# Routing tiles of a gated cross-attention and expert block: GpSimd's root, the probability transposes, the list columns and ScalarE's Exp each move within their queues

## What is computed

```python
kv = (ctx @ W_kv.T + b_kv).reshape(B, S, 16, 16, 2)          # k and v, 16 heads of 16
scores = einsum('bshd,bstd->bsht', layernorm(x), k) / 4      # over the heads t of one token
x = x + tanh(g0) * (einsum('bsht,bstd->bshd', softmax(scores), v) @ W_out.T + b_out)
xn = layernorm(x)
probs = softmax(einsum('ntd,ed->nte', xn, gate_w))           # 8 experts
g, m = top_k(probs.transpose(0, 2, 1), 64)                   # each expert takes 64 of 256 tokens
h = gelu(xn[m] @ w1[e]) @ w2[e]
x = x + tanh(g1) * scatter_add(g * h, m)
```

## Time and profile before

| | us |
|---|---|
| median of 3 runs | 764.04 |
| lowest and highest | 762.25, 764.85 |
| profiled execution, its time | 766.51 |
| profiled execution, its span | 764.5 |
| mean granted TensorE clock | 0.912 |

### The profile page before, as it was taken

One profiled execution on the slowest core, in us unless ns is written; L12 is line 12 of the kernel. 1 busy time (PEld: TensorE's weight loads), 2 busy tenths in 40 slices (PEclk: granted clock), 3 DMA queues, 4 the chain that ended last, 5 costly groups with the idle time before them and its releaser, 6 DMA issues.

```text
span 764.5 us, 10848 instructions
## 1 busy us (share of the span) xinstructions
PE 647.5 (85%) x3592; PEld 517.6 (68%) x3592; DVE 630.2 (82%) x894; ACT 388.3 (51%) x882; POOL 579.4 (76%) x497
## 2 busy tenths in 40 slices
PE   5678867453689999984999999859999999999994
PEld 2234433221478888873878888747888889999994
DVE  5899999997999999967999999859999743567672
ACT  5466656432466666733666666535665542323321
POOL 3899989996877999867898889858899833445443
PEclk9877898755699999996999999977999999999998
DMA  6877755230347878764688887536777878899982
GB/s 192 311 237 252 263 203 200 103 132 27 111 152 222 244 231 244 214 182 126 189 243 253 247 232 226 186 89 191 233 225 220 238 227 281 286 306 317 304 252 27
DMA packets 97069, 160.91 MB, mean 210 GB/s; under 512 B 8171, under 2 KB 74486, under 8 KB 97014
## 3 DMA queue, kind: packets, MB, share of 16 engines
q1 hardware_dynamic: 84150, 142.91, 56.1%
q0 software_dynamic: 12288, 16.79, 11.6%
q10 hardware_dynamic: 576, 0.52, 0.2%
HBM read 126.63 MB, written 33.55 MB: 210 GB/s over the span
## 4 chain that ended last, share of the span: by engine, by line
PE 55%; POOL 19%; DVE 8%; DMA 7%; issue 7%; ACT 3%; POOLq 0%; ACTq 0%; DVEq 0%
PE bank L1010 20%; PE bank L991 20%; POOL prod_p L313 9%; DMA out_dram<-ys,ids 7%; POOL tree_a L319 5%; PE bank L918 4%; DVE prod_v L456 3%; PE bank L938 3%; POOL tree_b L319 3%; PE bank L901 2%; PE bank L979 2%; POOL tree_c L319 1%; DVE co L458 1%; PE bank L950 1%; PE bank L927 1%
## 5 line engine op out<-in xcount | busy, mean ns | idle before, releaser
L991 PE MATMUL bank<-xin,w1in 128*128 128x256 f32 x1536 | 210.3, 296 | 5.5 <-DVE xin L592 3.8
L991 PEld LDWEIGHTS bank<-xin,w1in 128*128 128x128 f32 x1536 | 199.5, 202 | 7.2 <-issue 6.8
L1010 PE MATMUL bank<-w2s,hT 128*128 128x256 f32 x768 | 175.4, 382 | 0.0
L379 POOL DMA_INDIRECT out_dram<-ys,ids x64 | 110.0, 1719 | 75.6 <-ACT ys L747 57.9
L1010 PEld LDWEIGHTS bank<-w2s,hT 128*128 128x128 f32 x768 | 142.4, 190 | 17.7
L737 ACT ACTIVATE hT<-bank 128x512 f32<-128x512 f32 x128 | 76.4, 597 | 118.5 <-PE bank L991 118.1
L313 POOL TENSOR_TENSOR prod_p<-kvs,q 128x1024 f32<-128x1024 f32 (+2 forms) x32 | 99.8, 3118 | 13.0 <-ACT q L704 12.9
L458 DVE TENSOR_REDUCE co<-prod_v 128x192 f32<-128x3072 f32 (+1 forms) x32 | 104.6, 3270 | 1.1
L456 DVE TENSOR_TENSOR prod_v<-bank,Ex 128x3072 f32<-128x3072 f32 (+1 forms) x32 | 104.5, 3265 | 0.1
L456 DVE TENSOR_TENSOR prod_v<-bank,q 128x3072 f32<-128x3072 f32 (+2 forms) x32 | 95.5, 2983 | 6.3 <-ACT q L704 6.3
L365 POOL DMA_INDIRECT xg<-xn_scratch,ids x64 | 65.0, 1016 | 46.1 <-DVE ids L582 28.6
(11 more groups left out here) (118 smaller groups left out, 1044.9 us busy)
## 6 DMA issues: line engine op xcount, KB each, us to landing
w1in<-w_parts SPq DMA_DIRECT2D x128, 512.0 KB, 5.4
w2s<-in_L_ffn_w_dram SPq DMA_DIRECT2D x32, 1024.0 KB, 6.2
w_parts<-w1s SPq DMA_DIRECT2D x32, 512.0 KB, 3.4
w1raw<-in_L_ffn_w_dram SPq DMA_DIRECT2D x32, 256.0 KB, 4.3
ct<-in_ctx_dram SPq DMA_DIRECT2D x32, 128.0 KB, 5.3
xt<-in_x_dram SPq DMA_DIRECT2D x32, 128.0 KB, 4.2
out_dram<-x SPq DMA_DIRECT2D x32, 128.0 KB, 4.2
xn_scratch<-xn SPq DMA_DIRECT2D x32, 128.0 KB, 2.7
```

The source lines that it names most:

```text
L379: pool.indirect_dma_start(out=out_rows[:, :], out_offset=bass.IndirectOffsetOnAxis(ap=ids[:, g % 2, p * E + e:p * E + e + 1], axis=0), in_ ...
L991: ins = pe.matmul(HB[k % 2][:, D * f:D * (f + 1)], w1in[:, k, w, c, P * f:P * (f + 1)].bitcast(f32r), xin[:, n % 2, x_, c, :], start=(m == ...
L1010: ins = pe.matmul(dst, hT[:, n % 2, f, cols], w2s[:, n % 2, f, :], start=(f == 0), stop=(f == FC - 1))
```

## The change

Only the order of calls in the routing tiles changes, and one instruction of each choice of tokens goes. GpSimd: rsqrt(s + 1) stands ahead of scores(s). VectorE: residual(s - 1) stands behind Sc, ahead of routes, as in other tiles; the last match_replace of a choice, whose result nobody reads, is left out. ScalarE: take_y stands behind the Exp, and the Exp's table is loaded by a one-column Exp (`exp_warm`) behind make_q. TensorE: prob_transposes stands ahead of hidden(n, 0), and route_columns ahead of outputs(n - 1, 1); in tile 10 prob_transposes stands ahead of co_transposes, and xn_transposes and logits ahead of route_columns. The loops of ScalarE and TensorE are written anew with the routing tiles apart; the order of other tiles is as it was.

```diff
 # GpSimd
             for s in range(NT):
+                if routing(s):
+                    rsqrt(s + 1)
                 scores(s)
-                rsqrt(s + 1)
+                if not routing(s):
+                    rsqrt(s + 1)
 # VectorE
-                if t > 0 and not routing(t):
+                if t > 0:
                     residual(t - 1)
                 if routing(t):
                     routes(t // TG - 1)
...
                 products(hc, Vp, Ev[:, 0:hc, :], co[:, 0:hc * DK], 2 * t + 1, cov_done)
-                if t > 0 and routing(t):
-                    residual(t - 1)
...
-                    dve.max_index(top_i[:, eight], top_p[:, eight], work[:, :])
-                    dve.match_replace(work[:, :], top_p[:, eight], work[:, :], -1.0).then_inc(removed8, 1)
-                    wait_apart(removed8, n + 1)
+                    if r < CAP // 8 - 1:
+                        dve.max_index(top_i[:, eight], top_p[:, eight], work[:, :])
+                        dve.match_replace(work[:, :], top_p[:, eight], work[:, :], -1.0).then_inc(round_done, 1)
+                    else:
+                        dve.max_index(top_i[:, eight], top_p[:, eight], work[:, :]).then_inc(round_done, 1)
+                    wait_apart(round_done, n + 1)
 # ScalarE, a routing tile
+                    if n >= 0:
+                        take_ctT(s + 1)
+                        gelu(n, 0)
+                        gelu(n, 1)
+                    take_coT(s - 1)
+                    take_kv(s + 1)
+                    make_xn(s - 2)
+                    x_stats(s + 2)
+                    take_xnT(s - 2)
+                    if n >= 0:
+                        gelu(n, 2)
+                        gelu(n, 3)
+                    take_logits(s - 2)
+                    make_q(s + 1)
+                    act.activation(exp_warm[:, :], tanh_g[:, 0:1], ACT.Exp)
+                    exponentials(s)
+                    if n >= 1:
+                        take_y(n - 1)
+                    take_xh(n + 1)
 # TensorE, tiles from 10 on
+                if n >= 0 and s + 1 < NT:
+                    ctx_transposes(s + 1)
+                if routing(s):
+                    prob_transposes(s // TG - 1)
+                if n >= 0:
+                    hidden(n, 0)
+                    hidden(n, 1)
+                co_transposes(s - 1)
+                if s + 1 < NT:
+                    project_kv(s + 1)
+                project_out(s - 1)
+                if not routing(s):
+                    token_transposes(n + 1)
+                if n >= 1:
+                    outputs(n - 1, 0)
+                xn_transposes(s - 2)
+                if n >= 0:
+                    hidden(n, 2)
+                    hidden(n, 3)
+                logits(s - 2)
+                if routing(s):
+                    route_columns(s // TG - 1)
+                if n >= 1:
+                    outputs(n - 1, 1)
+                if routing(s):
+                    token_transposes(n + 1)
```

More of the change, by code:

```diff
@@ L814, in _ @@
                 n = s - N0
-                if n >= 0 and s + 1 < NT:
-                    take_ctT(s + 1)
[L817 to L823, removed]
+                if routing(s):
[18 more added lines that the diff above has]
+                    take_xh(n + 1)
+                    continue
@@ L846, in _ @@
-                if s + 2 < NT and n < 0:
+                exponentials(s)
+                take_xh(n + 1)
+                make_xn(s - 2)
+                if s + 2 < NT:
                     x_stats(s + 2)
+                take_xnT(s - 2)
+                gelu(n, 2)
+                gelu(n, 3)
+                take_logits(s - 2)
                 if s + 1 < NT:
                     make_q(s + 1)
-                if routing(s + 1) and s <= NT + 1:
+                if routing(s + 1):
                     gate_exp(s // TG - 1)
-                if s < NT and routing(s):
-                    exponentials(s)
@@ L854, in _ @@
-                if 0 <= n + 1 < NE and routing(s):
-                    take_xh(n + 1)
-                if 0 <= n - 1 < NE and not routing(s):
+                if n >= 1:
                     take_y(n - 1)
@@ L1079, in _ @@
                         low_part(s, k)
-                if 2 <= s < N0 - 1:
+                if s >= 2:
                     logits(s - 2)
-                if s < N0 - 1:
-                    ctx_transposes(s + 2)
-                if n >= 0 and s <= NT + 1:
-                    logits(s - 2)
-                if routing(s) and s <= NT + 2:
-                    if 0 <= n - 1 < NE:
-                        outputs(n - 1, 1)
+                ctx_transposes(s + 2)
+            pe.wait_ge(low_made, Q * E)
+            for s in range(N0 - 1, NT):
+                n = s - N0
+                if n >= 0 and s + 1 < NT:
[6 more added lines that the diff above has]
+                co_transposes(s - 1)
+                if s + 1 < NT:
+                    project_kv(s + 1)
+                project_out(s - 1)
[9 more added lines that the diff above has]
+                if routing(s):
                     route_columns(s // TG - 1)
-                if s == N0 - 1:
-                    xn_transposes(s - 2)
-                    logits(s - 2)
-                if routing(s) and s <= NT + 2:
+                if n >= 1:
+                    outputs(n - 1, 1)
+                if routing(s):
                     token_transposes(n + 1)
-                elif 0 <= n - 1 < NE:
-                    outputs(n - 1, 1)
             n = n1 - 1
```

33 lines of the change are left out of this document (6 added, 27 removed).

## The result

The changed kernel takes 743.95 us (median of 4 runs, 743.56 to 745.63) against 764.44 for the kernel before, timed beside it (4 runs, 762.25 to 767.35). The ratio is 0.9734, with a 95% interval of 0.9698 to 0.977. The profiled execution took 744.05 us, with a span of 742.0. Twelve experiments follow; each has its own runs of the kernel before on its chip. One run of the kernel before, 874.17 us long at a granted clock of 0.717, is left out of all comparisons as slow.

What follows compares the result with a forecast made beforehand. Bound: TensorE, VectorE and GpSimd nearly full, except waits in routing tiles 10, 18 and 26. Gains of 4.9 + 8.7 + 8.7 = 22.3 us from the 764.04 median gave 741.7 us; range 738 to 749.5.

Steps and rivals of the forecast that it cites:

- Tile lengths: Routing tiles 10, 18 and 26 were to last 25.7, 27.3 and 27 us, from 30.6, 36.1 and 35.6.
- The root first: GpSimd's 0.72 us root ahead of scores in tile 18: hidden 2 and 3 begin at 333.82 instead of 336.65, without gap.
- One match_replace less: VectorE in tile 18: dropping the match_replace makes the lists 0.40 us sooner.
- Denominator 8.3 us sooner: VectorE in tile 18: with the Exp ahead of the output rows, the denominator starts at 340.3 against 348.60.
- Gather 7.0 us sooner: GpSimd in tile 18: with columns ahead of the second output pair, it gathers at 339.3 instead of 346.32.
- Gathered rows split 2.8 us ahead of low_tokens: Tile 18: ScalarE has split the gathered rows by 345.4; VectorE needs them at 348.2.
- rival 1: Gathers land late behind weight loads: 0.6 us for a tile, or 749.3 us if contention reaches 10 us; 12%.
- GpSimd is late next: After tile 18 GpSimd is 7.0 us sooner, 8.6 with its query wait used, against VectorE's 8.8; 8.7 taken.
- The drain of the Trainium skill's page: ScalarE's table load plus drain costs 2.66 us; as a rival, tiles 18 and 26 lose 1.28 us each, 744.3; 3%.
- the probabilities first: Tile 18: take_probs 1.23 us sooner; TensorE's tile waits behind the probabilities, ready within 0.1 us, costed at nothing.
- rival 4: Slower: late probabilities hold up TensorE's whole tile in tiles 18, 26 and 10; at 10 us each, 771.7 us; 2%.
- Tile 10: Routing tile without an expert: denominator 4.4 us sooner plus 0.5 for the residual, 4.9 us gained.

Runs made afterwards that it cites:

- probs_back: Changed kernel with the probability transposes behind hidden 0, 1 and the context transposes again, and the eighth match_replace of each pass back: 746.75 us, ratio 0.978.
- columns_only: Kernel before with only the list columns moved ahead of the second output pair in tiles 18 and 26: 767.33 us, ratio 1.0029.
- exp_only: Kernel before with only the Exp and its one-column preload moved ahead of the output rows in tiles 18 and 26: 760.95 us, ratio 0.9954.
- root_back: Changed kernel with GpSimd's root behind its scores again in the three routing tiles: 750.25 us, ratio 0.9838.

## Why the prediction was right

The sum put the profiled execution at 744.2 us and its span at 742.2; they were 744.05 and 742.0. The forecast against the median, 741.7, was 2.2 us low: of 22.3 us the medians show 20.5. The term that was off is the step from the one profiled execution to the median. The profiled execution of before was 2.5 us over its median, that of after 0.1 us over, and I had subtracted the whole sum from the median. The con rows from tile 9 to 31 give 22.4 us between these two traces, so the sum is right for the execution it was read from, and about 2 us of what that execution had too much lie inside this stretch: the start (167.4 us to con of tile 9) and the tail (156.2 us behind con of tile 31) are like those of the other traces (166.8 to 169.1, and 155.6 to 157.2).

The likely cause is the clock behind TensorE's gap of 2.5 us, in tiles 18 and 26. In the trace of before both were followed by half clock (4.53 and 4.40 us for hidden 2 and 3), in other traces some were followed by full clock (3.11), so that an execution of before may be up to 2.7 us shorter; I had counted all of this as gain. The 32 timings of the kernel before beside the experiments fit: 20 lie at 761.7 to 764.1 us with a mean granted clock of 0.917, one at 764.5, and 11 at 765.7 to 767.8 us with 0.912. The two slow stretches would lower the mean clock by an estimated 0.004, from their granted clocks of 0.64 and 0.67 over 4.5 and 4.4 us. It is not shown: there is only one trace of before.

Step by step, forecast first:

- Tile lengths 25.7, 27.3 and 27: 25.52, 27.29 and 26.80.
- take_probs right behind the score reduce: in tile 18 it starts at 320.61, 1.14 us behind the reduce's start at 319.47.
- The root first: ScalarE waits for it no more, and TensorE has no gap ahead of hidden 2 and 3, which run at full clock; the mean clock of tile 18 rose from 0.84 to 0.95.
- One match_replace less: 0.40 us forecast; the lists start 0.44 us behind the start of the last max_index, before 0.84.
- Wait for the columns under 0.5 us: none. Wait for the Exp 1 to 1.5 us: 1.37, 1.35 in tile 26. Denominator 8.3 us sooner: 18.49 us behind con instead of 26.79, 8.3.
- Gather 7.0 us sooner: 334.56 is 17.74 behind con of tile 17, where 346.32 was 24.51: 6.8.
- Gathered rows split 2.8 us ahead of low_tokens: 1.6 (341.59 to 343.23). Over all gathers the landing is 3.6 us in the median and 7.3 at most, before 3.4 and 6.8, so rival 1 cost nothing here.
- GpSimd is late next: it waited for no query any more in tile 20, and con of tile 19 waits 1.03 us for it. Its part of tile 18's 8.8 us was forecast at 0.1 to 0.2; tiles 19 and 20 took back 0.16 and 0.17, but over tiles 19 to 25 together it is only 0.06; behind tile 26, tiles 27 to 31 took back 0.55.
- The Exp follows its load at once again (333.48 + 1.28, next at 334.77), as rows 4 had it. The drain of the Trainium skill's page on ScalarE: Activation LUTs (What ACT_TABLE_LOAD costs) is not in this trace either.

One step inside the tiles was wrong. I cost the probabilities first at nothing on TensorE; in tile 26 it waits 0.67 us for them. A wait of more than a few tenths was the sign that I had named for being wrong there, and it is the mechanism of rival 4 at a small price: TensorE gains on VectorE in tiles 19 to 25 and arrives too soon, with its first row of tile 26 0.05 us behind con of tile 25 where it was 0.96. probs_back shows that it makes the tile 0.95 us longer, and that tile 27 gives it back. That tile 26 still came out near its 27 us is in part luck: TensorE's earlier start was not in the sum either, and with it and without the wait the tile lasts 25.85 us (probs_back).

Tile 10 came out as summed, and a little better. VectorE in tile 10 of the changed kernel:

```profile
183.60 0.38 DVE L586 TENSOR_TENSOR ids<-bank,row_base 64x16 uint32<-64x16 f32 x2
...
184.53 0.42 DVE L508 TENSOR_REDUCE den<-Ex 128x16 f32<-128x256 f32 x1
```

The start of ids reads 183.60 as in rows 7, but con of tile 9 is at 167.81 here and was at 167.43: the ids are 0.38 us sooner in the tile, the match_replace's time, and the residual ahead of them costs nothing, where I had let it cost 0.15. The denominator is 4.49 us sooner and the tile 5.01, forecast 4.4 and 4.9.

The five parts are one chain. Undone singly, the root costs 4.5 us, the Exp's place 7.8, the columns 5.1, probabilities with match_replace 1.3 and the residual 0.45 at con of tile 31, 19.1 together of 22.4; alone, against the long trace of before, the root brings 9.9, the Exp 5.9 (2.5 of them by the clock and by TensorE's earlier start in tile 26) and the columns -1.1. So what a part is worth depends on which of the others are there.

What stays open: what decides the clock behind the gap of 2.5 us, and with it how much of the change's 20.5 us is clock; and how the start and tail come to vary by 1 to 2 us from one profiled execution to the next. The match_replace by itself was not tried.

## What to carry to other kernels

A wait in the trace is no price: walk the new queue orders from one common start, engine by engine, and take the latest of the inputs at each meeting point; here that gave every routing tile to 0.2 us, while the waits' own lengths (5.84, 6.27 and 2.02 us) were worth 2.75 us (tile 18), 2.5 (tiles 18 and 19) and 4.7 (tile 18) when their parts were undone. Walk every such tile by itself where an engine may come to it sooner than before, as TensorE did in tile 26. And find out where the one profiled execution stands among the timed ones before you subtract its waits from their median. Of two waits on one path, moving one alone can bring nothing or a loss, as columns_only did, so test such parts together. And before pricing a clock gap or a stall behind the changed place, ask which engine is full there: with GpSimd full behind each routing tile, 1.5 us of matmul time vanished, and of 1.79 us of GpSimd work 1.6 came through. A gain can also end at a transfer: 0.8 of 0.9 us of Exp did in tile 18, at the gathered rows.

## What the hardware showed that I had not expected

One and the same gap of 2.53 to 2.56 us on TensorE, ahead of the same 24 matmuls, stands eight times in four traces:

| kernel, tile | hidden 2 and 3, us | granted clock in them |
|---|---|---|
| before, 18 and 26 | 4.53, 4.40 | 0.64, 0.67 |
| columns_only, 18 and 26 | 4.60, 4.31 | 0.63, 0.68 |
| exp_only, 18 and 26 | 4.40, 3.11 | 0.67, 1.00 |
| root_back, 18 and 26 | 3.11, 3.12 | 1.00, 1.00 |

In the first of them the clock is 0.62 and 0.53 in the two windows of 2 us from 336 to 340 and 1.00 from 340 to 342: half clock and then full within the row. So five were followed by a stretch of half clock and three by none, and the same gap cost 1.2 to 1.5 us or nothing. A memset of 128 x 2048 bf16 on GpSimd took 1.79 us.
